# A network layer's normalisation and fp4 rounding of its first four tiles, moved into the phase before

## The reference

```
x  = x + s * silu(ffn0(xn))                 # end of layer 0
xn = (x - mean(x)) / sqrt(var(x) + 1e-5)    # layer norm of layer 1
def fp4_quant_dequant(x):                   # blocks of 16 along the row
    scale = max(|x|) / 6, at least 1e-12
    return nearest of {0, .5, 1, 1.5, 2, 3, 4, 6} to |x| / scale, * sign * scale
gate = fp4(xn) @ fp4(w_gate).T ; y = fp4(xn) @ fp4(w_up).T       # 704 wide
h    = silu(gate) * y
out  = fp4(h) @ fp4(w_down).T
s    = retention(xn) ;  x = x + s * silu(out)
```

## Time and profile before

| | |
|---|---|
| runs | 1718.71, 1723.58, 1724.39 us; median 1723.58 |
| the profiled execution | 1735.17 us, its span 1733.4 us |
| busy, share of span | PE 78%, PEld 55%, DVE 80%, ACT 70%, POOL 68% |
| combining | first instruction 659.7, last of DVE ends 885.3 |
| norm and feed-forward | first load 890.0, last of ACT ends 1310.4 |

### The profile page before, as it was taken

The page is one execution under the profiler, slowest core; times in us unless marked ns, Lnnn a source line. Parts: engine busy times, 40 slices in busy tenths (PEclk is TensorE's granted clock), DMA queues, the critical chain, the costliest instruction groups (busy, mean ns, idle before and its releaser), DMA issues. The chain is left out here.

```text
span 1733.4 us, 63737 instructions
## 1 busy us (share of the span) xinstructions
PE 1356.7 (78%) x21833; PEld 952.4 (55%) x21834; DVE 1388.8 (80%) x3713; ACT 1215.3 (70%) x3356; POOL 1181.3 (68%) x1299
## 2 busy tenths in 40 slices
PE   3539999979999982244517999999987899999857
PEld 2515555558777761123314666666664566666646
DVE  7878877768787864888858999999974688888748
ACT  7818888858777772566657888888744677777645
POOL 6838888744343446777416999999874687787747
PEclk9999999989999996567668999999999999999969
DMA  8727777779989895666634666666552122222238
GB/s 255 237 89 175 208 203 194 190 167 189 206 202 210 200 192 179 192 214 204 199 110 91 137 129 127 131 128 132 105 111 52 47 50 53 54 51 52 50 104 292
DMA packets 495356, 256.27 MB, mean 148 GB/s; under 512 B 359357, under 2 KB 484864, under 8 KB 494720
## 3 DMA queue, kind: packets, MB, share of 16 engines
q1 hardware_dynamic: 482658, 219.11, 52.3%
q0 software_dynamic: 12576, 35.67, 6.5%
HBM read 79.52 MB, written 73.44 MB: 88 GB/s over the span
## 5 line engine op out<-in xcount | busy, mean ns | idle before, releaser
L242 PE MATMUL ps<-all_late,l_xq_T 128*128 128x352 f16 x1536 | 253.1, 317 | 55.0 <-DMA l_xq_T<-l_apart 35.1
L242 PEld LDWEIGHTS ps<-all_late,l_xq_T 128*128 (+1 forms) x1536 | 147.0, 99 | 147.4 <-DVE ffn_h L829 39.1
L242 PE MATMUL ps<-l0moe_W,all_xT_all 128*128 128x16 f16 (+2 forms) x1152 | 190.4, 312 | 31.7 <-ACT all_xT_all L1038 22.4
L1611 POOL TENSOR_TENSOR all_late<-experts_se,all_mhalf 128x4 f32<-128x4 f32 (+1 forms) x77 | 76.3, 991 | 172.9 <-DVE experts_se L1801 164.0
L242 PE MATMUL ps<-l_Wq,all_xT_all 128*128 128x256 f16 x384 | 76.1, 357 | 124.3 <-DVE both_y L2066 92.9
L2463 POOL TENSOR_TENSOR all_late<-ret_pm,all_late 128x512 f16<-128x512 f32 x128 | 145.5, 1158 | 19.4 <-ACT all_late L2369 19.4
L242 PEld LDWEIGHTS ps<-l0moe_W,all_xT_all 128*128 128x128 f16 x1152 | 83.3, 100 | 117.0 <-ACT all_xT_all L1038 26.0
L667 PE MATMUL ps<-all_late,ffn_hT 128*128 128x256 f16 x1088 | 131.6, 276 | 9.7 <-ACT l_xq_T L731 6.2
L242 PEld LDWEIGHTS ps<-l_Wq,all_xT_all 128*128 128x128 f16 x384 | 45.3, 124 | 147.0 <-DVE both_y L2066 98.0
L667 PEld LDWEIGHTS ps<-all_late,ffn_hT 128*128 128x128 f16 x1088 | 106.7, 99 | 30.0 <-issue 7.4
L242 PE MATMUL ps<-moe_E,experts_gT 128*128 x864 | 115.3, 274 | 0.0
(11 more groups left out here) (308 smaller groups left out, 4601.0 us busy)
## 6 DMA issues: line engine op xcount, KB each, us to landing
rows_dram<-all_late SPq DMA_DIRECT2D x72, 256.0 KB
ret_v<-ret_vpad SPq DMA_DIRECT2D x256, 64.0 KB
front_xin<-x SPq DMA_DIRECT2D x16, 512.0 KB
x_dram<-front_x SPq DMA_DIRECT2D x16, 512.0 KB
all_late<-x_dram SPq DMA_DIRECT2D x64, 128.0 KB
z_dram<-all_late SPq DMA_DIRECT2D x64, 128.0 KB
both_zin<-z_dram SPq DMA_DIRECT2D x16, 512.0 KB
both_xin<-x SPq DMA_DIRECT2D x16, 512.0 KB
```

Source lines behind the costliest of these rows:

```text
L242: mm = pe.matmul(out, lhs[a], rhs[b], start=first and n == 0, stop=last and n == 2, skip_group_check=True)
L1611: pool.tensor_tensor(rows[:, n % 4, which, :, 0], se[:, u, which], power[:, which], ALU.pow).then_inc(s_time, 1)
```

## The change

The first group (four tiles, `HEAD` = 4) is normalised and rounded while combining still runs. Group 0 has been stored in round 4; SP loads it again in round 5 (`both_hx`). ACT sums rows in round 7 and squares in round 9, POOL does the small powers in rounds 9 and 11, ACT normalises and makes the upper half in round 11, DVE finds the fp4 scale in round 12 (after its own work of that round), ACT takes Abs at the end of round 13, DVE rounds in round 14, POOL makes the lower half of `xn` in round 16, and in round 17 SP transposes `xn` into `all_xT_all` and ACT makes the upper half of the rounded `xn`; POOL makes its lower half after its last round. SP stores that (512 KB, `headq_dram`) after the last result. The working area of the rounding is two pairs of PSUM banks.

In the next phase the four rounded tiles are read back by transposing DMAs, two ahead of the first load. The norm pipeline runs over tiles 4 to 63, `K` is 7 instead of 11, and `scheduled(..., 4, 16, 11)` unrolls 16 steps and makes 11 passes, where `pipeline` unrolled 24 and made 10.

```diff
-    half, both, K, U = FF // 2, 2 * FF // P, 11, 2
-    PAIRS = TILES // U
+    half, both, K, U = FF // 2, 2 * FF // P, 7, 2
+    NORMED = TILES - HEAD
+    PAIRS, BEHIND = NORMED // U, HEAD // U
...
+            def turn_head(n):
+                sp.dma_start_transpose(xq_T[:, n], head_tiles[n]).then_inc(s_head[n], 16)
...
+            turn_head(0)
+            turn_head(1)
+            stages = [(0, NORMED, even(load)), (6, NORMED, even(turn_x)), (9, NORMED, even(turn_q)), (K + 6, TILES, turn_h)]
+            for s in range(TILES + K + 6):
...
+                if 2 + s < HEAD:
+                    turn_head(2 + s)
... phase_combine ...
+        hq = Quant(ph, "hq", G * D, 1.0, work=[ps[:, 0:2, :].rearrange("p b k -> p (b k)"), ps[:, 2:4, :].rearrange("p b k -> p (b k)")])
+        HEAD_LOAD, HEAD_SUM, HEAD_MEAN, HEAD_SQUARE, HEAD_ROOT, HEAD_NORM, HEAD_SCALE, HEAD_LOW, HEAD_TURN, HEAD_QUANT = (
+            5, 7, 9, 9, 11, 11, 12, 16, 17, 17)
+            for h in range(HEAD_GROUPS):
+                sp.wait_ge(hq.lo, LAG + h + 1)
+                sp.dma_start(token_groups(headq_dram)[h], hq16[:, h]).then_inc(s_hstored[h], 16)
...
+            def head_squares(h):
+                for g in range(G):
+                    ins = act.activation(hjunk[:, g], hx[:, h, g], ACT.Square, bias=haway[:, h, g:g + 1],
+                                         accum_out=hsquare[:, h, g:g + 1])
+            def head_low(h):
+                pool.wait_ge(s_hhi, h + 1)
+                pool.tensor_tensor(h16[:, h, :, D:2 * D], hx[:, h], h16[:, h, :, 0:D], ALU.subtract).then_inc(s_hlo, 1)
+            def head_scale(h):
+                dve.wait_ge(s_hxn, h + 1)
+                hq.dve_amax(dve, t, rows)
+                hq.dve_step(dve, t)
+                hq.dve_reciprocal(dve, t)
+                hq.dve_scale(dve, t, rows)
+            def head_round(h):
+                hq.dve_round(dve, t)
+                hq.dve_grid(dve, t)
+                hq.dve_value(dve, t)
```

More of the change, by code:

```diff
@@ L86 @@
 PACK1W = _at
+HEAD_GROUPS = 1
+HEAD = HEAD_GROUPS * G
 GUW = C * 2 * 2 * FF
@@ L597, in phase_norm_ffn @@
         stage = nq.val[:].rearrange("p u k -> p (u k)")
+        s_head = [ph.sem(f"head{n}") for n in range(HEAD)]
         s_xin, s_turn, s_qturn, s_hT = (ph.slot_sems(n) for n in ("xin", "turn", "qturn", "hT"))
@@ L605, in phase_norm_ffn @@
         x_pairs = x_dram.rearrange("(n k p) d -> n p k d", k=U, p=P)
+        head_tiles = token_tiles(headq_dram)
         @block.sync
@@ L637, in turn_h @@
                     sp.dma_start(stage, jobs[1][0]).then_inc(s_stage[1], 16)
-            unrolled(TILES, [(0, even(load)), (6, even(turn_x)), (9, even(turn_q)), (K + 6, turn_h)], 4)
+            turn_head(0)
+            turn_head(1)
+            stages = [(0, NORMED, even(load)), (6, NORMED, even(turn_x)), (9, NORMED, even(turn_q)), (K + 6, TILES, turn_h)]
+            for s in range(TILES + K + 6):
+                for skew, many, work in stages:
+                    k = s - skew
+                    if 0 <= k < many:
+                        work(Tile(k, k % LAG, k // LAG, k % 4))
+                if 2 + s < HEAD:
+                    turn_head(2 + s)
             sp.wait_ge(s_const, 16 * len(loads))
@@ L797, in joined @@
             def joined(t):
-                return t.slot4 % 2 == 0 and not (isinstance(t.n, int) and t.n + NEAR >= TILES)
+                return t.slot4 % 2 == 0 and not (isinstance(t.n, int) and t.n + NEAR >= NORMED)
             def step(t):
@@ L1962, in _ @@
                     weights.pool_low(pool, low_at[i - 2])
+                if head_at(i, HEAD_MEAN) is not None:
+                    head_mean(head_at(i, HEAD_MEAN))
+                if head_at(i, HEAD_ROOT) is not None:
+                    head_root(head_at(i, HEAD_ROOT))
+                if head_at(i, HEAD_LOW) is not None:
+                    head_low(head_at(i, HEAD_LOW))
                 if group(i):
@@ L1968, in _ @@
                     gather_second(group(i), range(2, G))
+            for h in range(HEAD_GROUPS):
+                hq.low(pool, Tile(h, h, 0), hq16[:, h, :, 0:D], hq16[:, h, :, D:2 * D])
         @block.scalar
@@ L1974, in _, with head_sums, head_normalise, head_quantised @@
                 weights.act_magic(act, n)
+            hq.prime_act(act)
+            def head_sums(h):
+                act.wait_ge(s_hx[h], 16)
+                if h:
+                    act.wait_ge(s_hsum, h)
+                for g in range(G):
+                    ins = act.activation(hjunk[:, g], hx[:, h, g], ACT.Copy, accum_out=hsum[:, h, g:g + 1])
+                ins.then_inc(s_hsum, 1)
+            def head_squares(h):
+                act.wait_ge(s_haway, h + 1)
+                act.wait_ge(s_hsum, HEAD_GROUPS)
+                if h:
+                    act.wait_ge(s_hsq, h)
+                for g in range(G):
+                    ins = act.activation(hjunk[:, g], hx[:, h, g], ACT.Square, bias=haway[:, h, g:g + 1],
+                                         accum_out=hsquare[:, h, g:g + 1])
+                ins.then_inc(s_hsq, 1)
+            def head_normalise(h):
+                act.wait_ge(s_hshift, h + 1)
+                for g in range(G):
+                    ins = act.activation(hx[:, h, g], hx[:, h, g], ACT.Identity, scale=hrstd[:, h, g:g + 1],
+                                         bias=hshift[:, h, g:g + 1])
+                ins.then_inc(s_hxn, 1)
+                act.wait_ge(s_hxn, h + 1)
+                act.activation(h16[:, h, :, 0:D], hx[:, h], ACT.Copy).then_inc(s_hhi, 1)
+            def head_quantised(h):
+                act.wait_ge(s_y1, GROUPS)
+                hq.act_hi(act, Tile(h, h, 0), hq16[:, h, :, 0:D])
             def second_weighted(t):
@@ L2121, in _ @@
                 weights.dve_round(dve, n)
+            hq.prime_dve(dve)
             for i in rounds:
@@ L2141, in _ @@
                     weights.dve_scale(dve, scaled_at[i])
+                if head_at(i, HEAD_SCALE) is not None:
+                    head_scale(head_at(i, HEAD_SCALE))
+                if head_at(i, HEAD_SCALE + 2) is not None:
+                    head_round(head_at(i, HEAD_SCALE + 2))
 WRAP = 8
```

133 lines of the change are left out of this document (96 added, 37 removed).

## The result

The changed kernel takes 1726.88 us (median of 8 runs, 1724.27 to 1729.07), the kernel before in the same session 1723.49 (8 runs, 1718.71 to 1724.39). The ratio is 1.0024, 95% interval 1.0014 to 1.0034. The forecast was 1726.5 and "no difference", and the whole came out so. The parts did not all come out so, and that is what there is to learn.

A forecast was written before the change was run, and what follows sets the result against it. DVE was taken to bound both combining and norm and feed-forward. The terms 6.8 + 1.4 + 2.0 + 1.5 - 8.8 = +2.9 us on the median of 1723.6 gave 1726.5 us, "no difference", range 1719 to 1733.

The forecast's parts named there:

- DVE's head work: Combining, rounds 12 and 14: DVE's added instructions take 3.2 and 3.6 us, all on the path, +6.8 us.
- ACT's squares: Combining, round 9: four squares and a read exceed ACT's spare 0.71 us, passed to DVE in round 10, +1.4 us.
- The first block: Round 15: POOL's first 1024-column subtraction holds DVE about 2.7 us, taken up by DVE's 2.78 us wait for ACT.
- The second block: Round 17: POOL's second 1024-column subtraction holds DVE's inverse roots, which hold the gate of round 18, about +2.0 us.
- The second store: End of combining: the rounded tiles, 512 KB behind the last result's store on the same queue, cost +1.5 us.
- The start: Norm and feed-forward: first Silu 11.6 us earlier, less later first row sums because transposes precede the loads, -8.8 us.
- The loop: Norm and feed-forward: the interval per tile stays at 5.8 us, and one more loop pass costs nothing.
- The forecast's other form: The sum of +2.9 us added to the profiled execution of 1735.17 us instead of the median, giving 1738.1.
- POOL's gathers pace combining: Rival, combining: added DVE and ACT work and blocks fall into waits for gathered rows; -7.3 us, 1716.3, chance 0.12.
- all six POOL instructions block DVE: Rival, combining: each new POOL instruction stretches a DVE instruction, 8.7 us instead of 2.0; +9.6, 1733.2, chance 0.20.
- The rival's own mark: From 4.3 us of POOL blocks on DVE, the sum was to pass 5.2 us, the smallest difference that can be told.
- no block occurs by the issue order: Rival, combining: DVE issues first, so POOL's subtractions cost it nothing; +0.9 us, 1724.5, chance 0.13.

The follow-up runs named there:

- combine_only: The changed combining phase with the old norm and feed-forward phase behind it, which does not use what was prepared: 1735.29 us, ratio 1.0079 to the kernel before.
- squares8: The changed kernel with the head's squares and means in round 8 instead of 9 and the root in 10 instead of 11: 1723.71 us, ratio 1.0020.
- low_split: The changed kernel with POOL's first lower-half subtraction (128x1024) cut into four pieces of 128x256 in the same place: 1725.66 us in one run.
- low_dve: The changed kernel with the second lower half computed by DVE, in the round where it waits 1.2 us for ACT: 1723.40 us, ratio 1.0017.
- early_store: The changed kernel with the store of the rounded tiles issued in the last round ahead of the last result's store: 1724.14 us, ratio 1.0013.
- loads_first: The changed kernel with the next phase's first two loads of x issued ahead of the four transposes of the rounded tiles: 1722.38 us, ratio 1.0007.
- before_sems: The kernel before with 27 more, unused semaphores allocated in the combining phase: 1726.89 us in one profiled run.

## Why the prediction was right, and where it was not

The whole was right to 0.4 us, but with two errors that cancelled in part. That it came so close is luck: a block of 2.4 us was left out of the sum, squares were priced 0.75 too high, and the start earned more than its 8.8.

- *DVE's head work*, +6.8: rounds 12 and 14 grew by 3.20 and 3.66, together 6.86. Right, and on the path in full, as `combine_only` shows.
- *ACT's squares*, +1.4: the wait in round 10 grew by the forecast's mechanism, from 0.59 to 1.56, but the round only by 0.65. Oversized by half; `squares8` confirms the place.
- *The first block*, taken as hidden: this step failed. "The first falls in round 15, where the wait of 2.78 takes it up." The size, 2.7, was right (2.63 measured, 2.44 in the round), but the cover was not a property of the kernel. It was missing in the second profile of before and in that of the change. Nor was it there in `low_split`, on the chip where the kernel before shows it again: round 15 was 12.26 us. That is +2.4 which the sum doesn't have. The row that should have warned was there: ACT waited 4.83 us for nothing in the program, and I used this wait as a bound and a cover all the same.
- *The second block*, +2.0: 1.93, in the place named, and it goes when DVE does the work itself (`low_dve`). Right.
- *The second store*, +1.5: the boundary grew by 1.63, 1.6 of it by the landing of q behind the last result's (4.5 against 2.9 us after the last addition), some 0.1 to 0.2 by the clearing of more semaphores. Right, also in cause; `early_store` got only 0.83 back because its store of q still made the last one land later.
- *The start*, -8.8: -8.58 to the first Silu, -8.85 for the phase in this profile and about -10 by the five others. Right. The step of the sum that named four transposes ahead of the loads as a cost is confirmed by `loads_first`, which gets 3.2 us of it back at the Silu and about 3 over the whole kernel.
- The loop is unchanged: 5.8 us a tile before and after.

By rows of second profiles, the sum is 11.5 + 1.6 - 8.85 = +4.25 against the +2.9 forecast. The medians give +3.4, and with a phase shorter by 10 the sum would be 3. Against the one execution of the first profile, the same parts give only +0.4, for the 3.8 us by which its combining was longer than that of the second. The forecast's other form, 1738.1 for a profiled execution, missed the 1729.07 by 9 us: the 11.6 carried over from the first profile were that execution's own.

The rivals: that POOL's gathers pace combining is refuted, since none of the added DVE time was hidden. That all six POOL instructions block DVE was a third right: the two long ones did (4.4 us), the short ones did nothing that the rounds show. The rival's own mark was 4.3 us of blocks, and they came to 4.4; the change stayed "no difference" because the squares cost less than 1.4. That no block occurs by the issue order is refuted for these rows. The Trainium skill (SBUF — State Buffer, "Who interferes with whom") says that whoever issues first gets the shared ports and the other one waits. Whatever the engines' order inside the chip was, the profile's start times don't give it: behind a gather, a DVE instruction with two SBUF operands that began 0.46 to 0.66 us before POOL's subtraction was held. After idle time on POOL, the one that had ended as POOL's began (872.93) took its usual 0.17, and the next one, 0.03 after POOL's start, was held. The part of the page's rule that one operand in PSUM keeps DVE out of it agrees with L385 above.

## What to carry to other kernels

A wait that the profile puts down to nothing in the program is no cover: take a second profile before you hide work in it, or cost the work in full. Work moved off the front of one phase into the phase before is only earned where it lies in waits that are structural; here DVE's waits of 1.12 and 1.22 us for ACT in the last rounds took two instructions of 1.22 us for less than 0.1, while the same instructions on POOL cost 1.9 to 2.6 us each. Where the first transfers of a phase share a queue, issue those first whose results start the longest chain. A store issued 2 us ahead of the last one of a phase can still delay it, here by 0.6. And two single profiles of one phase differed here by 2 us, most of it through the granted clock, so a part is judged by several profiles or by the medians of the whole.

## What the runs showed beside

- ACT stands still for 2 to 8 us before single copies of transposed weights (L560, L562), with "remote" as the releaser. It was so in the first profile of before (6.75 and 4.83), in `before_sems` (8.12 and 4.67), in `low_split` (2.13), and in both profiles of the version without lower halves on POOL (2.56 and 3.14, then 3.26). It was in none of the other nine profiles. All eight of the first two sessions of experiments, on two chips where the kernel before takes 1721.7 to 1721.9 us, are without it; all four on two other chips, where it takes 1726.9 and 1731.3, have it. It goes with the chip rather than with the version, it seems, but the record doesn't name the chip of the first session, where one of two profiles had it, and each chip has few profiles. What releases ACT there was not found. Ratios of different sessions are not to be compared finely for that reason. The two rows are of ACT's timeline in `before_sems`.

```profile
789.32 0.81 ACT L560 ACTIVATE all_late<-ps 128x768 f16<-128x768 f16 x1 [8.12 <-remote]
846.92 1.02 ACT L560 ACTIVATE all_late<-ps 128x1024 f16<-128x1024 f16 x1 [4.67 <-remote]
```

- How long POOL's subtraction holds DVE goes with what POOL did before, in these rows. Directly behind a gather the hold begins about 0.5 us before POOL's record (2.63 for a subtraction of 2.13); after idle time it begins with it (2.11 for 2.12).
- Issuing the transposing load of the four normalised tiles held SP for 4.75 us, against 1.23 to 1.25 for one of the phase's own. In the last rounds SP has this time; ahead of a load it would not. The row is of the timeline of `low_dve`.

```profile
873.72 4.75 SPq L1966 DMA_TRANSPOSE all_xT_all<-both_h  x1
```
